# New orders, shorter MLP stages and constant products on TensorE in a transformer block for 16 sequences

## The chip, the cores and the metric

One core of one Trainium2 chip. The metric is the device time of one execution in microseconds. The engines are TensorE (PE; its weight loads are PEld), VectorE (DVE), ScalarE (ACT), GpSimd (POOL) and SyncE (SP), which here only issues DMAs.

## The reference, cut to what matters

For each of 16 samples x is 256 positions by 256 channels, with 16 heads of depth 16. Three residual blocks are modulated by a condition vector, and a fourth attends to the context:

```
m = silu(cond) @ w_ada + b_ada                       # 9 vectors of 256
h = ln(x) * (1 + sc) + sh;  x += g * (self_attn(h) @ w_so + b_so)    # "w": windows of 128, rolled by 64
h = ln(x) * (1 + sc) + sh;  x += g * (topk_attn(h, ctx) @ w_co + b_co)  # "t": softmax over the 16 largest of 256
h = ln(x) * (1 + sc) + sh;  x += g * (silu(h @ a) * (h @ b)) @ w_m2   # "m": 256 -> 2 x 1024 -> 256
x = x + attn(ada_ln(x), ada_ln(ctx)) @ Wp + bp        # "l": all 256 keys
```

## The kernel before

Nothing loops over the samples in the program order of an engine. Each sample is cut into some 230 stages, each stage belongs to one engine, and each engine runs its stages in an order that `orders()` sorts out of tables written by hand or by a planner: WINDOW (w), TOP (t), MIDDLE (m), LAST (l) and WEIGHTS give every stage a tick, `starts()` gives each sample its offset in each table, and SHIFTS moves single stages of samples 0 to 2 and 12 to 15. The ticks are only used for sorting. Semaphores hold the dependencies, so an order decides who waits, and not what is computed. In the middle of the run four samples are in work at once: the window part of sample b+1, the top-k part of b, the MLP of b-1 or b-2 and the last attention of b-3.

The stages that matter here, with the letter of the block behind the name and the number of the piece behind a colon:

- SP: `wd` weight chunk in, `xi` x in (three DMAs), `in_q`/`in_k` the stacks for the scores (six DMAs each), `gg` the guard row, `xo` out.
- PE: `wp` products with the condition (fp32), `x4` turns the normed x, `pj`, `vj` projections (12 products), `a` scores (4 or 8 products) into the bank pair `both_a`, `gd` turns the row maxima, `b` turned scores into `both_b` (for t with eight more products that add the `far` masks), `o` attention times values (fp32, 16 records in the profile), `ot`, `bk`, `xt` turns, `pr` output projection, `m1` and `m2` the MLP.
- DVE: `rm` row maximum of a score stage (1,024 columns at once, "pair instruction"), `t1` the eight largest and their removal for one bank, `t2` the next eight, `nv` division, `xa` residual add, `bn` statistics, `wl` the low part of a weight.
- ACT: `sp` scale and split into two fp16 halves, `e` exp over both banks of `both_b` ("pair instruction"), `os`, `fo`, `v`, `gc` copies, `mt`, `mh` of the MLP, `wh` the high part of a weight.
- POOL: `rs` norm, `lo` low half of a split, `fx` mask, `mp`, `ml` of the MLP.

`both_a` is one pair of banks for all score stages: stage n waits for `a_free >= 2 * (n - 1)`, which the last `rm` or `t1` on the one before gives. `t1:2k` and `t1:2k+1` read score stage `a_t:k`. The work banks (ND = 3) are taken in turn by `d_take`, in the order of TensorE's stages. `m1` has four stages a sample, each with two work banks and 24 products; `m2_0` has one stage of 48 products which waits for all four pieces of the hidden layer:

```
pe.wait_ge(hid_hi, HC // 2 * (b + 1))
pe.wait_ge(hid_lo, HC // 2 * (b + 1))
```

Weight chunks go through seven staging slots at first and later through three; the DMA of chunk i waits for the `wl` of the chunk that had its slot. `bank_c` is the bank of the `o` stages, of which they use the first 256 columns.

Of the kernel before, what the change touches and what calls it, by code (L numbers as in the profile page):

```python
# [12 lines left out]
P = 128  # L13
# [21 lines left out]
def by_depth(a, n):  # L35
# [11 lines left out]
    ("sp", "xi:0@-145.94128 in_wq:0@-27.37744 in_wk:0@-18.47637 gg_w:0@3.5209 gg_w:1@4.07101 gg_w:2@6.27184 "  # L47
            "gg_w:3@22.21006"),
    ("pe", "x4_n1:0@-9.09677 pj_wq:0@-1.98612 pj_wk:0@2.68519 vj_w:0@4.89993 a_w:0@24.58239 a_w:1@27.56313 "
            "gd_w:0@29.69328 gd_w:1@29.69488 a_w:2@30.1805 gd_w:2@33.0072 a_w:3@36.06898 b_w:0@37.52571 "  # L50
            "o_w:0@40.25652 b_w:1@40.44455 gd_w:3@40.44981 b_w:2@43.51234 o_w:1@45.50942 o_w:2@48.14002 "
            "b_w:3@48.47732 o_w:3@52.15513 ot_w:0@52.96945 bk_w:0@54.60357 pr_w:0@60.64486 xt_w:0@63.46943"),
    ("act", "sp_n1:0@-4.9099 sp_wq:0@0.03668 sp_wk:0@4.57516 v_w:0@7.99085 gc_w:0@30.25034 gc_w:1@31.91219 "
            "gc_w:2@35.31827 e_w:0@37.88181 os_w:0@39.82438 e_w:1@40.8623 gc_w:3@41.86752 e_w:2@45.6085 "
            "os_w:1@47.66581 os_w:2@49.63704 e_w:3@51.50998 os_w:3@53.88078 sp_ws:0@58.08033 fo_w:0@63.15316"),
    ("dve", "bn_n1:0@-31.7132 rm_w:0@25.42137 rm_w:1@27.82458 rm_w:2@29.82325 rm_w:3@36.91164 nv_w:0@56.27724 "
            "xa_w:0@66.96972"),
    ("pool", "rs_n1:0@-16.61517 lo_n1:0@-3.0515 lo_wq:0@3.04638 lo_wk:0@12.34686 lo_ws:0@60.30093"),
# [3 lines left out]
    ("sp", "ct:0@-99.6594 in_tk:0@-34.30848 in_tq:0@-24.27719 gg_t:0@14.98362 gg_t:1@23.54712 gg_t:2@34.21064 "  # L62
            "gg_t:3@52.14972"),
    ("pe", "pj_tk:0@-8.41414 x4_n2:0@1.63472 pj_tq:0@6.08886 a_t:0@23.94792 a_t:1@34.1613 a_t:2@40.7968 "
            "gd_t:0@41.76883 a_t:3@45.25534 b_t:0@45.59387 vj_t:0@51.57878 b_t:1@51.66042 gd_t:1@53.13278 "
            "a_t:4@54.9192 b_t:2@58.34345 a_t:5@59.57596 o_t:0@63.86381 gd_t:2@66.1775 a_t:6@67.38364 "
            "b_t:3@67.58863 o_t:1@71.25909 b_t:4@73.82902 a_t:7@75.59749 gd_t:3@81.92041 b_t:5@82.0796 "
            "b_t:6@86.37541 o_t:2@87.8269 b_t:7@88.51516 o_t:3@91.75181"),
# [1418 lines left out]
```

## Time and profile before

| | |
|---|---|
| three runs | 1408.02, 1410.12, 1412.46 us, median 1410.12 |
| the profiled execution | 1412.02 us; its span, first to last instruction, is 1409.4 us |
| mean granted TensorE clock | 0.951 |
| busy share of the span | PE 86%, DVE 82%, ACT 71%, POOL 62%, PEld 60% |
| products on TensorE | 13192 |

The span is the time of the traced instructions; 2.6 us of the execution lie around it. The page of the profile cuts the span in 40 slices of 35.2 us, and for each gives the busy share of each engine in tenths and the clock that TensorE was granted, in tenths of full speed (2.4 GHz; 5 would be 1.2 GHz throughout). The busy shares of the whole are means over a start, a long middle and an end which differ, so they are to be read by stretch.

### The profile page before, as it was taken

To read this page: it belongs to the slowest core of one execution; us is meant where nothing else is said; L and a number is where in the kernel's file an instruction comes from. 1 tells how busy PE (TensorE), PEld (TensorE's weight loads), DVE (VectorE), ACT (ScalarE), POOL (GpSimd) and SP (SyncE) were. 2 spreads that over 40 slices of the span, in tenths; PEclk is the share of its full clock that TensorE was granted. 3 is DMA by queue.
4 is the path that set the end of the run, shared out by engine and by line. 5 is a ranking of instruction groups with operands and counts; after the bars stand their busy time and mean duration, and the time that the engine had idled before them with its cause. 6 is when DMAs were issued, how large, how long until landed. Compare 5 with 4: busy or idle time off the path is not lost. (4 is left out here: it accounts for less than half of the span.)

```text
span 1409.4 us, 37816 instructions
## 1 busy us (share of the span) xinstructions
PE 1206.5 (86%) x13192; PEld 838.9 (60%) x13192; DVE 1155.1 (82%) x3823; ACT 994.4 (71%) x2001; POOL 878.4 (62%) x1161
## 2 busy tenths in 40 slices
PE   4647688989999999999999999999999989878765
PEld 4534365757666666666675766666666666555532
DVE  4339798989999999999999999999999999894322
ACT  3434476869687887869686969788787868576643
POOL 1133376958677685858585867768585848575610
PEclk9667799999999999999999999999999999999986
DMA  5411111202112120302021111112120211000010
GB/s 203 129 47 45 39 35 36 69 24 53 41 42 60 40 62 13 86 12 74 19 70 32 50 51 44 50 39 69 27 60 19 54 36 45 20 24 23 17 31 16
DMA packets 111385, 67.17 MB, mean 48 GB/s; under 512 B 13836, under 2 KB 107870, under 8 KB 111198
## 3 DMA queue, kind: packets, MB, share of 16 engines
q1 hardware_dynamic: 111198, 64.76, 17.1%
q8 instruction: 107, 1.75, 0.5%
q14 instruction: 80, 0.66, 0.2%
HBM read 22.33 MB, written 4.19 MB: 19 GB/s over the span
## 5 line engine op out<-in xcount | busy, mean ns | idle before, releaser
L1210 ACT ACTIVATE prob<-turned_score 128x1024 f32<-128x1024 f32 x320 | 326.5, 1020 | 113.3 <-PE turned_score L920 109.3
L1437 POOL TENSOR_TENSOR pair<-full,pair 128x512 f16<-128x512 f32 x192 | 221.7, 1159 | 154.8 <-ACT pair L1184 151.0
L1443 POOL TENSOR_SCALAR far<-far 128x512 bf16<-128x512 bf16 x256 | 158.0, 617 | 131.1 <-DVE far L1372 114.4
L1355 DVE MAX8 top<-score 128x8 f32<-128x256 f32 x512 | 193.5, 420 | 26.6 <-PE score L920 26.1
L1358 DVE MATCH_REPLACE8 rest<-top,score 128x256 f32<-128x256 f32 x512 | 208.3, 415 | 0.0
L1372 DVE MATCH_REPLACE8 far<-best,rest 128x256 bf16<-128x256 f32 x512 | 205.7, 410 | 0.2 <-issue 0.2
L1345 DVE TENSOR_REDUCE rowmax_l<-score 128x4 f32<-128x1024 f32 x128 | 156.2, 1220 | 54.2 <-PE score L920 40.8
L920 PE MATMUL work<-pair_n,w_m_hi 128*128 128x256 f16 x1024 | 172.7, 274 | 0.9 <-ACT other L1240 0.7
L920 PE MATMUL work<-pair_n,w_m_lo 128*128 128x256 f16 x512 | 140.1, 274 | 0.0
L1184 ACT ACTIVATE pair<-full 128x512 f16<-128x512 f32 x192 | 121.0, 630 | 23.6 <-DMA q_stack_l<-pair 6.6
L1422 POOL TENSOR_SCALAR rstd_n<-mean_var_n 128x2 f32<-128x2 f32 x64 | 12.8, 200 | 175.2 <-DVE mean_var_n L1337 172.6
L1345 DVE TENSOR_REDUCE rowmax_w<-score 128x8 f32<-128x1024 f32 x64 | 78.1, 1220 | 40.2 <-PE score L920 29.8
L920 PEld LDWEIGHTS work<-pair_n,w_m_hi 128*128 128x128 f16 x1024 | 98.0, 98 | 18.6 <-issue 6.3
L1365 DVE MAX8 best<-rest 128x8 f32<-128x256 f32 x256 | 107.0, 418 | 0.0
L1367 DVE MAX8 best<-rest 128x8 f32<-128x256 f32 x256 | 104.8, 410 | 0.0
L920 PE MATMUL work<-hid,w_m_hi 128*128 128x256 f16 x512 | 86.9, 277 | 1.2 <-issue 1.2
L1452 POOL TENSOR_TENSOR gated<-gated,linear 128x512 f32<-128x512 f32 x64 | 81.3, 1270 | 5.0
L1398 DVE TENSOR_TENSOR x_tile<-x_tile,work 128x512 f32<-128x512 f32 x64 | 43.7, 683 | 49.2 <-PE work L917 40.1
L920 PE MATMUL turned_score<-ident,far 128*128 128x128 bf16 x1024 | 82.1, 225 | 0.0
L1449 POOL TENSOR_TENSOR linear<-linear,other 128x512 f32<-128x512 f32 x64 | 81.3, 1270 | 0.0
L1456 POOL TENSOR_TENSOR hid<-gated,hid 128x512 f16<-128x512 f32 x64 | 74.0, 1159 | 10.1 <-ACT hid L1250 7.1
L920 PE MATMUL score<-k_stack_l,q_stack_l 48*128 48x256 f16 x512 | 51.3, 279 | 31.5 <-DVE rowmax_l L1345 23.9
(197 smaller groups left out, 3149.6 us busy)
## 6 DMA issues: line engine op xcount, KB each, us to landing
q_stack_w<-pair SPq DMA_DIRECT2D x96, 64.0 KB, 2.3
k_stack_w<-pair SPq DMA_DIRECT2D x96, 64.0 KB, 2.3
k_stack_t<-pair SPq DMA_DIRECT2D x96, 64.0 KB, 2.3
q_stack_t<-pair SPq DMA_DIRECT2D x96, 64.0 KB, 2.3
k_stack_l<-pair SPq DMA_DIRECT2D x96, 64.0 KB, 2.3
q_stack_l<-pair SPq DMA_DIRECT2D x96, 64.0 KB, 2.3
ctx_t<-in_ctx_turned SPq DMA_DIRECT2D x16, 256.0 KB, 2.9
ctx_l<-in_ctx SPq DMA_DIRECT2D x16, 256.0 KB, 2.9
```

The lines of the kernel that those rows point to most:

```text
L920: return pe.matmul(o, lhsT, rhs, start=start, stop=stop)
L1184: act.activation(pair_tile(s, b)[:, 0, :, :], tile[:, :, :], ACT.Copy).then_inc(split_hi, 1)
L1210: act.activation(prob[:, at:at + 2, :], both_b[:, :, :], ACT.Exp).then_inc(exp_done, 1)
L1345: dve.tensor_reduce(rowmax[s][n % 2][:, :].rearrange("p (z m) -> p z m", z=2)[:, :, at:at + wide], both_a[:, :, :].rearrange("p z (h k) -> ...
L1355: first = [step(dve.max(eight[:, t, :], bank[:, t * L:(t + 1) * L])) for t in range(LT)]
L1358: m = dve.match_replace(rest[p % 2][:, t, :], eight[:, t, :], bank[:, t * L:(t + 1) * L], -FAR)
L1365: second = [step(dve.max(best[p % 2][:, 0, :], rest[p % 2][:, 0, :]))]
L1367: second.append(step(dve.max(best[p % 2][:, 1, :], rest[p % 2][:, 1, :])))
L1372: m = dve.match_replace(far[p % NFAR][:, t, :], best[p % 2][:, t, :], rest[p % 2][:, t, :], -FAR)
L1437: pool.tensor_tensor(pr[:, 1, :, :], whole[:, :, :], pr[:, 0, :, :], ALU.subtract).then_inc(split_lo, 1)
L1443: pool.tensor_scalar(tile, tile, FAR, -1.0, ALU.add, ALU.mult).then_inc(far_fixed, 1)
L1449: pool.tensor_tensor(linear[:, two, :], linear[:, two, :], other[:, two, :], ALU.mult).then_inc(pair_product, 1)
```

## The change

1. All tables, `starts()` and SHIFTS have new numbers, so that the orders differ on all five engines; SHIFTS now is given for the same samples. No stage is added or taken away but for those of point 2.
2. `m1` is 8 stages with 12 products and one work bank each, `m2` is 4 stages of 12 products: two column halves for the first four of the eight depth chunks, then two for the rest. It takes its bank in the first of them, and a semaphore of its own, `m2_done`, tells of the last.
3. `idle_work()`: before 34 named stages TensorE multiplies `ident16` by itself into unused columns of `bank_c`, 821 times in all, behind a wait for the copy of the latest `o` stage. 553 of them are in the fill (119 before wp:14, 24 before the first x4, 45 before the first pj), 268 in samples 13 to 15.

Vector's order in one steady period before, from the `xa_w` of sample b to the next (@0 is sample b):

```
xa_w@0 t1:8@-1 t1:9@-1 bn_n2@0 rm_l:0@-3 t2:8@-1 t2:9@-1 t1:10@-1 t1:11@-1 rm_l:1@-3 t2:10@-1 t2:11@-1 t1:12@-1
t1:13@-1 t2:12@-1 rm_l:2@-3 t2:13@-1 rm_l:3@-3 rm_l:4@-3 nv_l@-4 rm_l:5@-3 t1:14@-1 t1:15@-1 t2:14@-1 rm_w:0@1
bn_nc@-1 rm_w:1@1 t2:15@-1 rm_w:2@1 xa_l@-4 bn_n1@2 t1:0@0 t1:1@0 t2:0@0 t2:1@0 rm_l:6@-3 rm_w:3@1 xa_m@-2 bn_n4@-2
nv_t@-1 rm_l:7@-3 t1:2@0 t2:2@0 t1:3@0 t2:3@0 t1:4@0 xa_t@-1 t1:5@0 bn_n3@-1 nv_w@1 t2:4@0 t2:5@0 t1:6@0 t1:7@0
t2:6@0 t2:7@0
```

and after:

```
xa_w@0 t1:9@-1 t2:8@-1 rm_l:0@-3 bn_n2@0 t2:9@-1 t1:10@-1 t1:11@-1 t2:10@-1 rm_l:1@-3 t2:11@-1 t1:12@-1 t1:13@-1
rm_l:2@-3 rm_l:3@-3 t2:12@-1 rm_l:4@-3 nv_l@-4 rm_l:5@-3 t2:13@-1 t1:14@-1 t1:15@-1 t2:14@-1 rm_w:0@1 t2:15@-1
rm_w:1@1 xa_l@-4 rm_w:2@1 bn_nc@-1 t1:0@0 t1:1@0 t2:0@0 rm_l:6@-3 t2:1@0 rm_w:3@1 xa_m@-2 nv_t@-1 bn_n4@-2
rm_l:7@-3 bn_n1@2 t1:2@0 t1:3@0 t2:2@0 t2:3@0 t1:4@0 xa_t@-1 bn_n3@-1 t1:5@0 nv_w@1 t2:4@0 t2:5@0 t1:6@0 t1:7@0
t2:6@0 t2:7@0 t1:8@0
```

In the fill, SP's order begins `wd:0 .. wd:9 xi:0 wd:10 ..` before and `wd:0 .. wd:13 xi:0@0 wd:14 .. wd:18 xi:0@1 wd:19 in_wq in_wk` after; VectorE's has `bn_n1` behind wl:5 before and behind wl:13 after; TensorE's has wp:14 behind `pj_wq` and wp:19 behind `a_w:2` before, and wp:14 in front of `x4_n1` and wp:19 in front of `a_w:0` after. At the end TensorE's order after has `m2:2 m2:3` of sample 14 between `b_t:7` and `o_t:3` of sample 15, where `m2_0` stood, and `m1:2` of sample 15 between `a_l:0` and `a_l:1` of sample 14.

The diff without the tables:

```diff
+IDLE_WORK = ("wp:0:14=119 x4_n1:0:0=24 pj_wq:0:0=45 wp:0:19=21 a_w:0:2=21 bk_w:0:0=18 pr_w:0:0=7 xt_w:0:0=17 "
+             "x4_n2:0:0=24 pj_tq:0:0=45 a_w:1:0=30 a_w:1:2=21 a_t:0:0=31 a_w:1:3=20 bk_w:1:0=25 pr_w:1:0=43 "
+             "a_t:0:4=10 a_t:0:7=25 a_t:1:0=7 bk_t:15:0=10 x4_n4:14:0=15 xt_t:15:0=17 a_l:14:3=15 bk_l:13:0=8 "
+             "xt_m:15:0=17 x4_n4:15:0=34 pj_lq:15:0=17 a_l:15:0=26 bk_l:14:0=8 a_l:15:3=9 a_l:15:7=14 "
+             "o_l:15:3=17 bk_l:15:0=18 pr_l:15:0=43")
...
-                   ("x4", "pj", "vj", "gd", "ot", "bk", "pr", "xt", "m1", "m2", "wp")]
-        d_keys = [k for k in d_users for _ in range(2 if k[0][:2] in ("ot", "m1") else 1)]
+                   ("x4", "pj", "vj", "gd", "ot", "bk", "pr", "xt", "m1", "wp") or k[0] == "m2" and k[2] == 0]
+        d_keys = [k for k in d_users for _ in range(2 if k[0][:2] == "ot" else 1)]
...
+            idle, o_begun = idle_work(), 0
             for piece, b, i in plan["pe"]:
                 kind, _, s = piece.partition("_")
+                if (piece, b, i) in idle:
+                    if o_begun > 0:
+                        pe.wait_ge(osum_done, o_begun)
+                    for _ in range(idle[piece, b, i]):
+                        mm(bank_c[:, L:L + P], ident16[:, :], ident16[:, :], True, True)
...
-                    for j in range(2):
-                        bank, n = d_take(piece, b, i, back=1 - j), 2 * i + j
-                        three_terms(bank[:, 0:L], W["m1"], slice(n * P, (n + 1) * P), own_pair["n3"], CC)
-                        m = three_terms(bank[:, L:2 * L], W["m1"], slice(HID + n * P, HID + (n + 1) * P),
-                                        own_pair["n3"], CC)
+                    bank = d_take(piece, b, i)
+                    three_terms(bank[:, 0:L], W["m1"], slice(i * P, (i + 1) * P), own_pair["n3"], CC)
+                    three_terms(bank[:, L:2 * L], W["m1"], slice(HID + i * P, HID + (i + 1) * P), own_pair["n3"],
+                                CC).then_inc(d_ready, 1)
+                elif kind == "m2":
+                    if b == 0 and i == 0:
+                        pe.wait_ge(lo_done, weight_count("m2"))
+                    c, half = i % 2, i // 2
+                    pe.wait_ge(hid_hi, HC // 2 * b + 2 * half + 2)
+                    pe.wait_ge(hid_lo, HC // 2 * b + 2 * half + 2)
+                    bank = d_take(piece, b, i) if i == 0 else d_bank("m2", b, 0)
+                    for k in range(HC // 2 * half, HC // 2 * (half + 1)):
+                        for n, (a, part) in enumerate((("hi", 0), ("hi", 1), ("lo", 0))):
+                            m = mm(bank[:, c * L:(c + 1) * L], W["m2"][a][:, k, c * P:(c + 1) * P], hid[:, part, k, :],
+                                   i == 0 and k == 0 and n == 0, i == 3 and k == HC - 1 and n == 2)
+                    if i == 0:
                         m.then_inc(d_ready, 1)
-                elif kind == "m2":
-                    if b == 0:
-                        pe.wait_ge(lo_done, weight_count("m2"))
-                    pe.wait_ge(hid_hi, HC // 2 * (b + 1))
-                    pe.wait_ge(hid_lo, HC // 2 * (b + 1))
-                    bank = d_take(piece, b, i)
-                    for c in range(CC):
-                        m = three_terms(bank[:, c * L:(c + 1) * L], W["m2"], slice(c * P, (c + 1) * P), hid, HC)
-                    m.then_inc(d_ready, 1)
+                    if i == 3:
+                        m.then_inc(m2_done, 1)
```

## Rows read from the trace of the kernel before

**Rows 1.** The page, the span in 40 slices: VectorE's busy tenths and TensorE's clock
```profile
DVE  4339798989999999999999999999999999894322
...
PEclk9667799999999999999999999999999999999986
```

**Rows 2.** The table by stretch: length, busy us of each engine, clock, DMA
```profile
42.00:69.30 27.30, 16.25 (x164) 12.25 (x164) 10.58 (x16) 10.51 (x17) 3.62 (x7) 0.55 0.44 133
120.50:170.00 49.50, 35.10 (x323) 21.92 (x322) 42.17 (x161) 21.72 (x41) 19.45 (x29) 0.78 0.19 49
605.90:681.90 76.00, 71.17 (x826) 49.77 (x818) 70.78 (x237) 60.97 (x125) 54.75 (x73) 1.00 0.18 47
1352.00:1409.40 57.40, 33.87 (x248) 16.06 (x248) 13.18 (x16) 18.35 (x30) 4.78 (x5) 0.68 0.11 28
```

**Rows 3.** VectorE's timeline, steady part: start, us, what, idle before and its end
```profile
642.47 0.69 DVE L1398 TENSOR_TENSOR x_tile<-x_tile,work 128x512 f32<-128x512 f32 x1 [0.80 <-PE work L917]
...
654.47 1.22 DVE L1345 TENSOR_REDUCE rowmax_l<-score 128x4 f32<-128x1024 f32 x1 [0.56 <-PE score L920]
...
667.97 1.23 DVE L1345 TENSOR_REDUCE rowmax_l<-score 128x4 f32<-128x1024 f32 x1 [0.55 <-issue]
...
718.46 0.69 DVE L1398 TENSOR_TENSOR x_tile<-x_tile,work 128x512 f32<-128x512 f32 x1 [0.76 <-PE work L917]
```

**Rows 4.** TensorE's timeline, steady part, end of an m1 stage and after
```profile
1100.68 0.27 PE L920 MATMUL work<-pair_n,w_m_lo 128*128 128x256 f16 x1
1100.88 0.39 PE L920 MATMUL score<-k_stack_l,q_stack_l 48*128 48x256 f16 x4
1101.21 0.39 PE L920 MATMUL work<-pair,w_qkv_hi 128*128 128x256 f16 x2
```

**Rows 5.** Timelines of SP, VectorE and ScalarE, the first 45 us
```profile
15.74 1.70 SPq L869 DMA_DIRECT2D x_tile<-in_x  x3
23.59 0.97 SPq L864 DMA_DIRECT2D hid<-in_L_xcond_w_m  x2
...
30.12 0.37 SPq L864 DMA_DIRECT2D hid<-in_L_xcond_w_m  x1
...
40.54 3.88 SPq L889 DMA_DIRECT2D q_stack_w<-pair  x6
...
21.57 0.75 DVE L1334 BATCH_NORM_STATS2 stats_n<-x_tile 128x6 f32<-128x256 f32 x2 [2.74 <-DMA x_tile<-in_x]
...
31.35 0.55 ACT L1176 ACTIVATE full<-work,ada 128x256 f32<-128x256 f32 x1
```

**Rows 6.** TensorE's timeline, the fill
```profile
34.50 0.58 PE L920 MATMUL work<-pair,w_qkv_hi 128*128 128x256 f16 x2 [7.39 <-POOL pair L1437]
...
38.33 0.38 PE L920 MATMUL work<-pair,w_qkv_hi 128*128 128x256 f16 x2
...
50.11 0.61 PE L920 MATMUL score<-k_stack_w,q_stack_w 48*128 48x128 f16 x8 [2.11 <-DMA k_stack_w<-pair]
...
54.82 3.44 PE L920 MATMUL work<-cond_T,hid 128*128 128x16 f32 x16
...
101.47 0.61 PE L920 MATMUL score<-k_stack_t,q_stack_t 48*128 48x256 f16 x4 [1.47 <-DVE rowmax_w L1345]
```

**Rows 7.** The chain that ended last: start, us, what
```profile
1275.07 1.84 PE work L920 x14
1276.91 1.04 PE attended L920 x16
...
1280.85 5.24 PE work L920 x48
...
1383.12 1.87 PE attended L920 x16
...
1401.69 3.50 PE work L920 x14
```

**Rows 8.** VectorE's timeline, its last MATCH_REPLACE8
```profile
1275.77 0.41 DVE L1372 MATCH_REPLACE8 far<-best,rest 128x256 bf16<-128x256 f32 x1
```

More of the change, by code:

```diff
@@ L46 @@
 WINDOW = (
[L47 to L58, printed above, removed]
+    ("sp", "xi:0@-149.05811 in_wq:0@-22.39374 in_wk:0@-21.63518 gg_w:0@-6.70743 gg_w:1@-6.20742 gg_w:2@3.72515 "
+            "gg_w:3@10.37658"),
@@ L59 @@
+    ("dve", "bn_n1:0@-17.84269 rm_w:0@24.47919 rm_w:1@26.55546 rm_w:2@29.71092 rm_w:3@39.32701 nv_w:0@54.92831 "
+            "xa_w:0@62.38605"),
+    ("pool", "rs_n1:0@-19.44322 lo_n1:0@-8.8718 lo_wq:0@3.49632 lo_wk:0@11.63506 lo_ws:0@54.42283"),
 )
 TOP = (
[L62 to L68, printed above, removed]
@@ new lines @@
+    ("pe", "pj_tk:0@-7.66208 x4_n2:0@1.34278 pj_tq:0@10.7192 a_t:0@24.62457 a_t:1@36.3855 a_t:2@40.46992 "
+            "gd_t:0@41.16911 b_t:0@46.39389 a_t:3@47.54705 b_t:1@49.06852 vj_t:0@49.42558 gd_t:1@52.91429 "
+            "a_t:4@53.28068 b_t:2@59.66427 a_t:5@60.56827 o_t:0@62.91677 a_t:6@66.51438 b_t:3@67.69902 "
+            "gd_t:2@68.67071 o_t:1@76.5107 b_t:4@79.63426 a_t:7@80.32481 gd_t:3@82.46194 b_t:5@83.04624 "
+            "o_t:2@85.87755 b_t:6@86.53666 b_t:7@89.11422 o_t:3@92.86888"),
@@ L109 @@
-    ("pool", "rs_nc:0@-31.49787 lo_nc:0@7.97103 rs_n4:0@9.40636 lo_n4:0@19.15097 lo_lk:0@22.80535 lo_lq:0@24.22699 "
-            "lo_ls:0@124.61473"),
+    ("sp", "cl:0@-113.28517 in_lk:0@-11.3877 in_lq:0@-8.30312 gg_l:0@8.54748 gg_l:1@30.92847 gg_l:2@34.1449 "
+            "gg_l:3@55.14878 xo:0@129.90888"),
+    ("pe", "x4_nc:0@-16.97885 x4_n4:0@14.3594 pj_lk:0@18.74146 pj_lq:0@20.78305 a_l:0@36.38003 a_l:1@41.1725 "
+            "vj_l:0@42.70583 gd_l:0@42.73227 a_l:2@49.44513 a_l:3@50.22124 b_l:0@50.82866 a_l:4@52.16861 "
+            "b_l:1@53.17633 a_l:5@54.31746 gd_l:1@54.80942 o_l:0@58.38301 gd_l:2@64.72824 a_l:6@67.98034 "
+            "b_l:2@68.09437 b_l:3@72.88562 a_l:7@73.99668 o_l:1@76.59819 b_l:4@79.41849 b_l:5@83.66516 "
+            "gd_l:3@87.4598 o_l:2@91.66504 b_l:6@98.85371 b_l:7@105.14574 o_l:3@107.70126 ot_l:0@117.03745 "
+            "bk_l:0@119.19155 pr_l:0@125.23099"),
@@ L512, in shifts, with idle_work @@
             found[stage, b, int(item)] = float(tick)
+    return found
+IDLE_WORK = ("wp:0:14=119 x4_n1:0:0=24 pj_wq:0:0=45 wp:0:19=21 a_w:0:2=21 bk_w:0:0=18 pr_w:0:0=7 xt_w:0:0=17 "
[3 more added lines that the diff above has]
+             "o_l:15:3=17 bk_l:15:0=18 pr_l:15:0=43")
+def idle_work():
+    found = {}
+    for one in IDLE_WORK.split():
+        name, _, n = one.partition("=")
+        stage, b, item = name.split(":")
+        found[stage, int(b), int(item)] = int(n)
     return found
@@ L731, in build @@
         hid_lo = sem("hid_lo")
+        m2_done = sem("m2_done")
         dve_own = sem("dve_own")
```

796 lines of the change are left out of this document (406 added, 390 removed).

## The prediction, made blind

> **What bounds the kernel now.** I read the page's slices first [rows 1]. VectorE is at 7 to 9 tenths from the fourth slice to the fifth from the end, and the granted TensorE clock is below full in two places only: the first 170 us and the last 60. So there are three stages with different limits: a fill, a steady part, a drain. The table by stretch gives each its numbers [rows 2]. In a steady period of 76.0 us (the same addition to x_tile starts at 642.47 and 718.46 [rows 3]) VectorE is busy 70.8 us and TensorE 71.2. VectorE is what sets the period: its order leaves it idle 5.2 us, and TensorE's own idle time is mostly waiting for VectorE to give back the score banks. In the fill TensorE is busy 16.3 of 27.3 us at a clock of 0.55, and in the last 57.4 us it is busy 33.9 at 0.68, with the other engines far from full: there a chain of latencies counts, and TensorE's part of it runs at half speed.
>
> How long half speed makes a step: 12 products of the same shape begin 0.21 us apart at 34.50 and 0.11 us apart at 38.33 [rows 6]. (The clock column has no record before 38 us and so says 1.00 there; the pace says half.) An `o` stage of sample 15 takes 1.87 us where one at full clock takes 1.04, and `pr_l` 3.50 against 1.84 [rows 7].
>
> **The steady part, orders.** All score stages share one pair of banks. After VectorE's last reading of it, the next `a` stage runs and VectorE reads again; if VectorE has nothing else between, it waits: 0.56 us at 654.47, 0.55 at 667.97 [rows 3]. Counting in the orders of `orders()`: before, 5 of the 20 score stages of a period follow each other on VectorE with nothing between; after, 2 do. (`rm_l:1`, `rm_w:3` and `t1:2` get a `t2` or a `bn` in front.) At 0.55 us each that is -1.6 us a period. The wait of `xa_w` (0.80 us at 642.47 [rows 3]) has `t1:8`, 1.5 us of work, moved in front of it; it may go, or be covered in half: -0.4. Against it: `rm_l:2` now comes directly behind `t1:13`, while TensorE has between `a_t:6` and `a_l:2` an `o`, a `b_t`, an x4, two small turns and half of the old `m1` (1.04 + 0.9 + 0.4 + 0.2 + 1.3 us and the score itself, some 4.1 us) where VectorE has only two `t1`, 2.9 us. So about 0.6 us beyond an ordinary turnaround, and I put another 0.4 for similar overruns at `a_l:1`, `a_l:5` and `a_w:1`. Net -1.6 - 0.4 + 1.0 = -1.0 us a period. Twelve periods lie between the add of sample 3 and that of sample 15: -12 us. From both sides: no wait comes back and both savings are whole, -2.4 a period, -29 us; the new waits are as large again as I think and none of `xa_w` goes, +0.4 a period, +5 us.
>
> **The steady part, smaller stages.** `m1` becomes 8 stages of 12 products, `m2` 4 of 12. The products are the same 1,536 and 768, and inside a stage a half costs nothing extra. What costs is a change of tiling: from products of 128 rows to score products of 48 rows the next start comes 0.20 us after the last instead of 0.11, and again on the way back [rows 4]. The old order has 63 such changes in a period, the new one 72: 9 x 0.1 = 0.9 us of TensorE. It has 4.8 us idle in a period [rows 2], so 3.9 are left, and the cover is VectorE; without it the price is 0.9 us a period, 11 us in all. The Trainium skill ("TensorEngine Tiling (Array Packing)", section Key Properties) says that changing the tiling mode drains TensorE, and speaks so against cutting stages finer between scores; the trace agrees with 0.1 us a change, and by the rule alone, with TensorE on the path, these steps would be +11 us where I count nothing.
>
> **The fill.** Fillers: 553 of the 821 constant products stand in the stages of samples 0 and 1 and the weights. None is in the trace of before; the nearest row is the eight 128-column bf16 products of `b_t` (0.055 us apart, 0.9 us with their four wide ones), so 30 us at full clock, 60 at half, spread over pauses. Each filler is behind a wait for the latest osum, which the next `o` would make anyway.
>
> First the order. `xi:0` moves on SP from behind wd:9 to behind wd:13. Before it was issued at 15.74 and `bn_n1` began at 21.57; wd:13 was issued at 30.12 [rows 5]. With `bn_n1` out of the weights' way, wd:10 (23.59 before) can go some 2.5 us earlier and wd:13 at about 27.3. Then x0 is issued by 29 and lands near 33, 11.5 us later. Not all of that is loss: before, `sp_n1` stood behind three weight copies on ScalarE and began only at 31.35 [rows 5], and `pj_wq` at 34.50. After: bn 33, x4 37.4, sp_n1 38, pj_wq 41.3, at full clock now, then in_wq from 45.7 against 40.54 [rows 5]. The 12 issues of in_wq and in_wk and the landing come behind it as before, so `a_w:0` is at about 55.3 against 50.11 [rows 6]: +5.2. The 119 fillers ahead of wp:14 begin at about 24.4, last 7 to 13 us, and end before or close to the time x is normed (37).
> From there: wp:19, 3.4 us between `a_w:2` and `gd_w:2` [rows 6], is moved ahead of `a_w:0`: -3.1. The other TensorE steps of sample 0's window attention, 42 to 69 us, halve where they are on the chain (some 3.5 us of the 16.3 busy). In the next stretch at half speed, before 101 us, `x4_n2` and `pj_tq` halve: -1.7. `a_t:0`, where VectorE becomes full, moves by 5.2 - 3.1 - 3.5 - 1.7 = -3.1 from 101.47 [rows 6]. From 120.5 to 170 VectorE is idle 7.3 of 49.5 us, against 3.4 at the steady rate, with TensorE's clock at 0.78 [rows 2]; half of the excess goes with the clock, -2. Fill: -5. Bounds: +5 (x late by all of 5.2, fillers do not lift the clock), -11 (x costs nothing).
>
> **The drain.** It is the 133 us behind VectorE's last MATCH_REPLACE8 [rows 8]. `m2` of samples 14 and 15 was 48 products, 5.24 us, in one piece [rows 7]. For sample 14 it stood between the last `b_t` of sample 15 and its last `o_t`; only half of it stands there now: -2.6. For sample 15 it stood behind the last `ml`; now the first half runs while GpSimd is at the later quarters: -2.6. `m1:1` of sample 15 was behind two scores that waited for in_lq's landing; its halves are now around one: -1.5. Then the clock: in the last 57.4 us TensorE is busy 33.9 at 0.68 [rows 2]. Summed over the chain, `pj_lq` 1.3, `pr_l` 1.7 twice, four `o` 0.8 each, `ot` 0.7, small ones 2: 10.6 us if all were at full clock. The 152 fillers of this stretch fill only parts of the pauses (26 products are 1.4 us in a wait of five), so I take half, -5. Drain: -12. Bounds: -4 (one half of `m2`, no clock, 43 fillers before the last `pr_l` 1.8 us too long at half clock) and -19.
>
> On the clock altogether there is a second estimate, which the sum does not use. The Trainium skill ("TensorE: Matmul & The Clock Gate", section Terms) prices throttled time at time x (1 - K/N); with the mean clock of 0.951 that is 69 us for the whole kernel, so up to -69 were TensorE always on the chain and all of it won. This trace does not agree that it all counts: TensorE is busy only 60% of such stretches [rows 2].
>
> **Sum.** The profiled execution took 1412.0 us, its span is 1409.4; the median of the three runs is 1410.1, 1.9 less. 1412.0 - 12 - 5 - 12 = 1383.0, less 1.9: 1381.
>
> **Rivals.**
> 1. *Only the ends gain.* The steady order trades five turnarounds for overruns and tiling changes, and the period stays at 76.0. For it: VectorE's and TensorE's loads are equal to 0.4 us, so every stage moved earlier makes another later. Against: the adjacent waits are plain in the rows. 1410 - 17 = 1393.
> 2. *The fillers do not lift the clock and only the order gains.* For it: they are in short groups, and the clock stayed at 0.55 with TensorE 60% busy. Against: the longest, 119 and 24 and 45, stand where TensorE was empty for 7.4 us. Fill +5, drain -7, steady -12: 1396.
> 3. *Slower: TensorE becomes the bound of the period.* Its work goes to 72.1 us; with stages that wait for their inputs at the head of its queue, scores come late for VectorE. It decides from +1.4 us a period, when 12 periods eat the 17 us of the ends; at +2.3 the time is 1410 - 17 + 28 = 1421. For it: 5.2 us of VectorE's idle time is already waiting for TensorE. Against: three more of the twenty scores have cover on VectorE than before, and `o_l:3`, 1 us of TensorE, now stands behind `a_t:6` and no longer in front of it.
> 4. *The whole gain.* -2.4 a period, -11 and -13 at the ends: 1357.
>
> **How the numbers follow.** The forecast 0.50; rival 1 0.17, rival 2 0.10, rival 3 0.14, rival 4 0.09. The likeliest alone spans 1368 to 1392. Leaving out most of rival 3 and the far side of rival 4 gives 1357 to 1405. 0.3%, 4 us, is what a measurement can tell from no change. Slower is rival 3 with its point of decision passed, 0.11; within 0.3% is its remainder and the edge of rival 2, 0.06; faster the rest, 0.83.
>
> **What would show it.** Right: a steady period of 75 us, VectorE's waits before `rm_l:1`, `rm_w:3`, `t1:2` and `xa_w` gone and one of about 1 us before `rm_l:2`; the first window score near 55 us but `a_t:0` near 98; a clock near 1 from about 30 us to 170 us; a last stretch, from the last MATCH_REPLACE8 to the end, of 121 us against 133. Wrong: a period of 76 or more, `a_t:0` after 101, or a clock in the last 57 us still under 0.8.

## The result, and the profile after

The changed kernel takes 1349.97 us (median of four runs, 1343.52 to 1354.03) where the kernel before takes 1409.54 beside it: ratio 0.957 [0.953, 0.961]. Run once more in a later comparison it took 1348.1 (five runs, 1342.23 to 1352.33), ratio 0.954 [0.951, 0.957]. So it is 60 us faster, where I predicted 29 and where my range ended at 1357. The profiled execution, the fastest of the first four, has a span of 1341.7 us and a mean granted clock of 0.977. It is set against the 1409.4 us span of before; some 8 of those 68 us are chance, since this execution was 6.4 us under the median of its kernel and that of before 2.5 over.

The page of after, its 40 slices (of 33.5 us); for [rows 1]:

```profile
DVE  4418999989999999999999999999999999896322
...
PEclk9888999989999999999999999999999999999998
```

The same stretches by event, first in before, then in after: up to the first top-k score `a_t:0`, to the residual add `xa_w` of sample 3, to that of sample 15, to VectorE's last MATCH_REPLACE8, to the end. The columns are length, then busy us of PE, PEld, DVE, ACT and POOL with their instructions, granted clock, DMA share and GB/s.

```profile
0.00:101.50 101.50, 55.01 (x400) 44.55 (x402) 35.30 (x71) 38.36 (x65) 23.82 (x40) 0.79 0.42 131
101.50:262.10 160.60, 123.67 (x1329) 85.29 (x1330) 143.58 (x544) 95.37 (x192) 88.34 (x123) 0.86 0.15 39
262.10:1178.20 916.10, 851.93 (x9792) 597.76 (x9789) 851.89 (x2845) 728.50 (x1488) 656.72 (x865) 1.00 0.18 46
1178.20:1276.20 98.00, 84.40 (x876) 56.30 (x877) 89.89 (x312) 67.82 (x137) 66.84 (x84) 0.97 0.08 21
1276.20:1409.40 133.20, 91.49 (x802) 54.98 (x799) 34.40 (x55) 64.39 (x121) 42.65 (x52) 0.85 0.09 23
```

```profile
0.00:104.90 104.90, 75.93 (x821) 67.91 (x822) 35.79 (x71) 38.13 (x65) 20.49 (x35) 0.89 0.43 132
104.90:255.50 150.60, 124.56 (x1462) 88.25 (x1461) 144.22 (x549) 96.08 (x193) 90.45 (x127) 0.94 0.14 38
255.50:1129.70 874.20, 849.75 (x9775) 593.88 (x9775) 841.50 (x2839) 725.89 (x1480) 651.06 (x858) 1.00 0.19 48
1129.70:1228.20 98.50, 88.73 (x942) 58.91 (x939) 91.19 (x314) 71.05 (x146) 71.77 (x93) 0.98 0.10 26
1228.20:1341.70 113.50, 94.32 (x1024) 65.82 (x1022) 33.68 (x51) 63.62 (x119) 41.41 (x51) 0.95 0.10 25
```

Read the first column down: +3.4, -10.0, -41.9, +0.5, -19.7 us (the last boundary of after lies 0.2 us early, so the last two are nearer +0.7 and -19.9). In the other profiled execution of the changed kernel, 1352.33 us long, the same five are +8.3, -6.3, -39.4, -0.1 and -21.4. So 60 to 67% of the gain is in the twelve periods of the middle, where the mean clock is 0.99 to 1.00 before and after; the fill differs by 5 to 9 us between the two profiles. And the first stretch became *longer*, though its clock went from 0.79 to 0.89 (0.83 in the other profile).

One steady period of after on VectorE, from `xa_w` to where the next has already begun; every line with a wait before it stands here, so this is all that is left of [rows 3]:

```profile
618.62 0.68 DVE L1439 TENSOR_TENSOR x_tile<-x_tile,work 128x512 f32<-128x512 f32 x1
...
636.67 1.22 DVE L1386 TENSOR_REDUCE rowmax_l<-score 128x4 f32<-128x1024 f32 x1 [0.86 <-issue]
638.46 1.23 DVE L1386 TENSOR_REDUCE rowmax_l<-score 128x4 f32<-128x1024 f32 x1 [0.56 <-PE score L947]
...
654.99 1.23 DVE L1386 TENSOR_REDUCE rowmax_w<-score 128x8 f32<-128x1024 f32 x1 [0.38 <-PE score L947]
```

These are `rm_l:2`, `rm_l:3` and `rm_w:2`, 1.8 us together; the period is 72.1, and in before it was 76.0 with 5.1 us of waits. The 3.3 us of waits that went are most of the 3.9. The other 0.6 us wasn't traced; an estimate is that six waits fewer save some 0.5, since an instruction of VectorE that doesn't wait starts about 0.08 us before the last one is over (a row maximum takes 1.22 us and the next starts after 1.14). What VectorE waited for over four periods, before and then after (total us, times, longest):

```profile
DVE top L1355 <- PE score L920: 6.7, 12, 0.7
DVE x_tile L1398 <- PE work L917: 4.6, 8, 0.8
DVE rowmax_l L1345 <- PE score L920: 2.4, 4, 0.8
DVE rowmax_w L1345 <- PE score L920: 2.2, 4, 0.6
DVE rowmax_l L1345 <- issue: 2.2, 4, 0.5
DVE recip L1386 <- PE work L917: 2.1, 4, 0.5
```

```profile
DVE rowmax_l L1386 <- issue: 3.7, 4, 1.1
DVE rowmax_l L1386 <- PE score L947: 2.2, 4, 0.6
DVE rowmax_w L1386 <- PE score L947: 1.5, 4, 0.4
```

20.2 us became 7.4. Not only waits for a score went: the adds (`xa_w`, `xa_t`) and the divisions (`nv`) waited 6.7 us for TensorE's products and wait no more. TensorE's side of the same four periods, before and after:

```profile
PE score L920 <- DVE rowmax_l L1345: 9.0, 20, 0.8
PE turned_score L920 <- ACT prob L1210: 3.8, 11, 0.7
PE score L920 <- DVE rowmax_w L1345: 1.7, 4, 0.4
```

```profile
PE work L944 <- POOL normed L1471: 2.6, 4, 0.7
PE work L944 <- DVE attn L1431: 1.1, 3, 0.6
```

In before TensorE stood 24 times in these four periods in front of a score because VectorE's row maximum of the last one wasn't done; in after not once. The two engines had been waiting for each other by turns.

### The profile page after: what moved, and what is told of

It is laid out like the page before. It is cut to its first block and busy times, and to the rows that moved or that the text cites. A ratio compares the mean times of both kernels' runs of the same rounds, so it can differ in the third digit from the quotient of the medians.

```text
span 1341.7 us, 39506 instructions
## 1 busy us (share of the span) xinstructions
PE 1233.3 (92%) x14013; PEld 874.8 (65%) x14013; DVE 1146.4 (85%) x3819; ACT 994.8 (74%) x2001; POOL 875.2 (65%) x1161
## 3 DMA queue, kind: packets, MB, share of 16 engines
q1 hardware_dynamic: 111198, 64.76, 17.9%
## 5 line engine op out<-in xcount | busy, mean ns | idle before, releaser
L1386 DVE TENSOR_REDUCE rowmax_w<-score 128x8 f32<-128x1024 f32 x64 | 78.0, 1219 | 36.7 <-PE score L947 19.7
L1406 DVE MAX8 best<-rest 128x8 f32<-128x256 f32 x256 | 106.7, 417 | 0.0
L947 PEld LDWEIGHTS turned_score<-ident,far 128*128 128x128 bf16 x1024 | 58.6, 99 | 27.8 <-issue 26.0
```

The costliest lines, as they stand in the source:

```text
L947: return pe.matmul(o, lhsT, rhs, start=start, stop=stop)
L1386: dve.tensor_reduce(rowmax[s][n % 2][:, :].rearrange("p (z m) -> p z m", z=2)[:, :, at:at + wide], both_a[:, :, :].rearrange("p z (h k) -> ...
L1406: second = [step(dve.max(best[p % 2][:, 0, :], rest[p % 2][:, 0, :]))]
```

## Experiments

Stages are given as in `orders()`; moves are for all steady samples. A period is the distance of the same `xa_w` add in two samples. "Run 3" is the experiment with number 3. Times are medians, with the ratio to the kernel before beside it and its 95% interval; the medians of before lay between 1409.85 and 1411.99.

**1. The constant products taken out, and only those of the end taken out.**

```diff
-            idle, o_begun = idle_work(), 0
+            idle, o_begun = {}, 0                                                    # e1
+            idle, o_begun = {k: n for k, n in idle_work().items() if k[1] < 3}, 0    # e2
```

> The changed kernel without its 821 constant products; orders and MLP stages stay. If the constant products hold the clock up and that is worth about a fifth of the gain, the steady period stays at 72.1 us, the clock in the fill and in the last 57 us falls back to 0.6 to 0.7, and the time rises by 8 to 15 us, to 1358 to 1365. Rival: the orders gave the ends as well, the constant products only fill waits, and the time stays within 4 us of 1350.

> The changed kernel with the constant products of samples 0 to 2 and the weights alone. Theory A (each end gains by its clock): about 4 us slower than the changed kernel, the last stretch at half clock as it is without any of them, from t2:15 to the end 119 us instead of 115. Theory B (the latency chain of the drain doesn't feel the clock): within 2 us of the changed kernel.

> The changed kernel once more, beside the next three on one chip. It gave 1349.97 us (1343.52 to 1354.03). Theory A (the constant products are worth the 12 us that its profiled execution shows beside the one without them): its median here lies 8 us or more under 1354.2. Theory B (they are worth 4 us, and the one profiled execution was a good one): 1348 to 1352.

Without any 1354.23 us (0.958 [0.956, 0.961]), with those of the fill alone 1354.45 (0.961 [0.958, 0.963]), with all 1348.1 and 1349.97. So the constants are worth 4 to 6 us of the 60 by the medians, all of it at the end, and 2 to 6 by the ratios; the interval without them overlaps both intervals with them, so the size is not well known. The stretch from the last `t2` to the end is 119.5 us without them and 114.8 with. In the fill the first top-k score comes earlier in some executions only. This is `a_t:0` of the same kernel in its other profiled execution:

```profile
109.82 0.39 PE L947 MATMUL score<-k_stack_t,q_stack_t 48*128 48x256 f16 x4
```

109.8, as late as without any constants (109.85), where the first profile had 104.9. Of the profiles here that share this start and these constants, seven have `a_t:0` at 104.5 to 106.7 and four at 108.1 to 109.8; with the constants of the fill alone it is at 109.55.

**2. The new orders with every MLP piece back in one place.** `m1:4` and `m1:5` adjacent, and all of `m2` where `m2:3` stands.

> The changed kernel with the pieces of the MLP put back together on TensorE: m1 0 and 1, 2 and 3, 4 and 5, 6 and 7 stand directly behind each other, and so do the four of m2, in the place of the last. If the smaller stages are what lets TensorE serve the scores in time, the steady period goes back by 2 us or more of the 3.9 won (74 to 76 us, time 1375 to 1395). If the order of VectorE did it, the period stays within 0.8 us of 72.1, and only the end loses up to 5 us: 1350 to 1364.

1429.70 us, ratio 1.012 [1.010, 1.015]: slower than before, with a period of 78.5. VectorE's waits over four periods:

```profile
DVE rowmax_w L1414 <- issue: 21.9, 4, 5.9
DVE rowmax_l L1414 <- PE score L975: 7.5, 5, 1.8
```

`rm_w:3` waits 5.1 to 5.9 us each time: all of `m2`, 5.2 us, stands in front of its score. That was too coarse a test (the place was the wrong one), so the next two put the pieces together one kind at a time and in the better place.

**3. `m2` whole in front of `a_l:6`; `m1` in pairs.**

```diff
+    for b in range(1, B - 3):                                    # m2 whole
+        pieces = [("m2", b, n) for n in range(4)]
+        at = order.index(("m2", b, 1))
...
+        order[at:at + 1] = pieces
...
+        for n in (0, 2, 4, 6):                                   # m1 in pairs, another run
+            order.remove(("m1", b, n))
+            order.insert(order.index(("m1", b, n + 1)), ("m1", b, n))
```

> The changed kernel with m2 in one piece again for samples 1 to 12, in the place of its second piece, in front of a_l:6. Between a_t:0 and a_l:6 TensorE then has about 6.4 us of work where VectorE has 4.4. If it is the TensorE work between two scores that must fit into VectorE's work between them, rm_l:6 waits 2 us and the period goes to 74: 1370 to 1378. If only the place in the run before last mattered (the pieces pushed a_w:3 back there), the period stays at 72.1: 1350.

> The changed kernel with only m1 in pairs again (m1:4 directly in front of m1:5, behind a_l:2). By the same rule rm_l:2 waits less by up to 0.9 us and rm_l:3 more by 1.3 us, so the period is 72.1 to 72.9 and the time 1350 to 1360: m2's pieces carry the gain and m1's hardly anything. Rival: both matter alike, 1365 or more.

`m2` whole: 1375.63 (0.976 [0.973, 0.979]), period 74.0, a new wait of 1.86 us before `rm_l:6`. `m1` in pairs: 1357.32 (0.962 [0.960, 0.965]), period 72.8, `rm_l:3` waits 1.84 instead of 0.56 and `rm_l:2` 0.55 instead of 0.87. In the new orders cutting `m2` is worth 26 to 28 us and cutting `m1` 7 to 9, where I had put both at nothing in the middle.

**4. The covers in the old orders.** The kernel before, with `rm_l:1` behind `t2:10`, `t2:1` behind `rm_l:6` and `bn_n1` behind `rm_l:7`, which is what the change does on VectorE with the three covers I priced.

```diff
+    turned("dve", ("rm_l", 1), ("t2", 10), -2)
+    turned("dve", ("t2", 1), ("rm_l", 6), 3)
+    behind("dve", ("bn_n1", 0), ("rm_l", 7), 5)
```

> The kernel before with three moves on VectorE alone, in all samples: rm_l:1 behind t2:10, t2:1 behind rm_l:6, bn_n1 behind rm_l:7, so that three score stages get work between them and the one before. If each uncovered turnaround costs its 0.55 us, the steady period falls from 76.0 to 74.4 and the time by 19 us, to 1390. Rival: the wait only goes elsewhere, since TensorE is the one that is late; period 75.5 to 76.5 and time within 5 us of 1410.

1440.91, ratio 1.019 [1.016, 1.022]: 29 us *slower* than before, with a period of 78.5. Over four periods:

```profile
DVE top L1375 <- PE score L940: 13.1, 12, 2.1
DVE rowmax_l L1365 <- issue: 11.3, 8, 2.3
DVE x_tile L1418 <- PE work L937: 4.7, 8, 0.8
DVE recip L1406 <- PE work L937: 2.5, 4, 0.7
```

The three turnarounds are gone, and `rm_l:6` waits 2.27, `t1:12` 2.13 instead of 0.69, and `t1:4` 0.65. The first has a plain reason: all of `m2`, 5.2 us of TensorE, stands in front of the score of `rm_l:6`, and the move took `t2:1`, 1.46 us of VectorE, from in front of it.

**5. The two heads in the old orders**: `t1:8` in front of `xa_w`, `a_t:6` in front of `o_l:3`.

> The kernel before with two swaps, in the steady samples: t1:8 of sample b-1 in front of xa_w of sample b on VectorE, and a_t:6 in front of o_l:3 on TensorE. They aim at the waits of 0.78 us (before xa_w) and 0.69 us (before t1:12). If they simply go, the period falls to 74.5 and the time by 18 us, to 1392. Rival: something behind them waits instead; then the period stays within 0.5 us of 76.0.

1410.24, ratio 0.998 [0.997, 1.000], period 75.8: the waits before `xa_w` and `t1:12` went, and 0.70 before `rm_l:0` and 0.65 before `rm_l:2` came.

**6. The new code with the old orders**: `m1` and `m2` pieces side by side where the whole stages stood, only `a_l:6` between the halves of `m2`, no constants; then the same with the moves of 4 and 5.

> The orders of before with m1 and m2 in pieces that stay together, but a_l:6 between the halves of m2 in the steady samples; no constant products. VectorE had work enough in front of rm_l:6 already, so by the rule of what fits between two scores the period stays at 76.0, at best 75.5: 1400 to 1412. If the small pieces gain by themselves, 1390 or less.

> The same with the three moves on VectorE and the two swaps of the runs before, which gave +2 % and nothing without the pieces. If pieces and order only pay together, rm_l:6 no longer waits 2.3 us and t1:12 no longer 2.1: the period falls to 74 or 75 and the time to 1380 to 1398, well under the kernel before. If the moves are bad in themselves, it stays over 1420.

1411.24 (1.001 [1.000, 1.003]) and 1417.71 (1.006 [1.004, 1.008]), periods 76.2 and 76.3. Neither the code of the small stages nor these moves with it bring anything in the old orders. But the pieces take back 23 of the 29 us that the covers of run 4 cost: with `a_l:6` inside `m2`, `rm_l:6` no longer waits and `t1:12` waits 1.13, while `rm_w:3` waits 1.24.

**7. The covers taken off in the new orders**, the mirror of 4.

```diff
+    turned("dve", ("t2", 10), ("rm_l", 1), 2)
+    turned("dve", ("rm_l", 6), ("t2", 1), -3)
...
+        order.remove(("bn_n1", b, 0))
+        order.insert(order.index(("t1", b - 2, 0)), ("bn_n1", b, 0))
```

> The changed kernel with the three covers taken off on VectorE alone: rm_l:1 in front of t2:10, t2:1 in front of rm_l:6, bn_n1 back in front of t1:0. Theory 1 (the prediction's: a score stage that follows its neighbour directly costs 0.55 us): +1.6 us in each of 12 periods, 1370, a period of 73.8. Theory 2 (a cover is worth what TensorE's work between two score stages exceeds VectorE's between their readings, counted in the new order): rm_l:1 moved off t2:10 leaves 4.4 us of TensorE's work against 2.9, +1.2 at rm_l:1; the place before rm_l:6 is 3.8 us against 5.8, nothing, but rm_w:3 then waits 3.0 against 1.1, +1.5; rm_l:7 to t1:2 2.2 against 1.1, +0.8: +3 us or more a period, 1385 or more, a period of 75.

1377.81 (0.976 [0.973, 0.979]), period 74.4 to 74.8. The same three moves that cost 29 us in the old orders are worth 28 to 30 in the new ones. Theory 2 had the direction and the places, but was 7 us too high: `rm_l:1` waits 1.4 to 1.6, and `rm_w:3` and `t1:2` only 0.55 and 0.62.

**8. The two heads taken back in the new orders, alone and with the covers.** `t1:8` behind `xa_w`, `bn_n3` behind `t1:5`.

> The changed kernel with t1:8 behind xa_w and bn_n3 behind t1:5 again, on VectorE alone. Theory 1 (the work in front hides the late products): the 0.77 us before xa_w and the 0.37 before xa_t come back, +1.1 a period, 1362, a period of 73.2. Theory 2 (TensorE's products for them come earlier by themselves, as it waits less for the score banks): less than 0.3 a period comes back, 1348 to 1353.

> The changed kernel with the three covers off and the two heads back (t1:8 behind xa_w, bn_n3 behind t1:5), on VectorE alone. Theory 1 (the late products before xa_w, nv_w and xa_t follow from TensorE's own waits): with TensorE waiting 4.7 us a period as without the covers, the waits before xa_w and its like are 0.5 us or more, a period of 75 or more, 1386 or more. Theory 2 (they come from the order of other engines): at most 0.2 us before them, a period of 74.4 as without the covers, 1376 to 1381.

Alone 1353.93 (0.959 [0.956, 0.961]), the period 72.2 nearly as it was, 0 to 0.28 us before `xa_w` in place of the 0.77 of before; the 4 to 6 us over the changed kernel are not in the period, and the intervals overlap. With the covers off too 1377.96 (0.976 [0.974, 0.978]), against 1377.81 without: again nothing, with 0 to 0.41 before `xa_w`. So it isn't mainly the work in front that removed the waits of the adds; TensorE's products for them come earlier against VectorE in the new orders, even with both engines waiting for each other again (4.2 us a period on VectorE).

**9. Two moves with a price by counting**: `t2:12` from `rm_l:4` to `rm_l:2`; `o_l:3` back in front of `a_t:6`.

> The changed kernel with t2:12 in front of rm_l:2 and no longer in front of rm_l:4. The largest wait left, 0.86 us before rm_l:2, gets 1.46 us of work in front. Theory 1 (each wait by itself): rm_l:2 0, rm_l:4 0.55, rm_l:3 0.59 as before: -0.3 a period, 1345. Theory 2 (a count of both engines' work between score stages, carried from one to the next): rm_l:4 waits 0.84 and rm_l:5 0.51, rm_l:3 0.5: +0.8 a period, +9 us, 1358.

> The changed kernel with o_l:3 in front of a_t:6 on TensorE again. Theory 1 (each by itself): t1:12 waits for the 1.25 us of o_l:3, rm_l:2 no longer waits: about +0.4 a period, +5 us. Theory 2 (the count, carried on): TensorE has 0.26 us and what it is ahead at a_t:6, the work is the same up to a_l:2, so the period moves by less than 0.15 and the whole by less than 2 us.

1350.51 and 1349.50 (both 0.955, [0.953, 0.958]), periods 72.35 and 72.28. The second is as counted: `t1:12` waits 0.59 again and `rm_l:2` 0.55 instead of 0.87. In the first the waits stand where the count put them (`rm_l:4` 0.72, `rm_l:5` 0.49, `rm_l:3` 0.56, none at `rm_l:2`), but cost 0.25 a period and not 0.8, so its 1358 was 7 to 8 us too high.

**10. The edits of runs 3, 7 and 8 together**: covers off and heads back, `m2` whole, `m1` in pairs, in the otherwise new orders.

> The changed kernel with covers and heads undone, and m2 in one piece and m1 in pairs besides. Theory 1 (each is a price of its own): +2.4 +1.9 +0.7 a period, 77.1, 1410. Theory 2 (the count of both engines' work between two score stages): undone covers put t2:1 in front of rm_l:6, which then covers the whole of m2, so m2 costs nothing more and m1 1.3 at rm_l:3: 75.7, 1393 to 1397.

1415.97 us, ratio 1.003 [1.001, 1.004]: 5 us longer than before. The twelve periods take 930.2 us, 56 more than in after and 14 more than in before; the last stretch keeps its gain (114.6), as `m2` stays cut in the last three samples:

```profile
263.90:1194.10 930.20, 859.62 (x9771) 601.05 (x9768) 846.76 (x2843) 725.39 (x1481) 651.89 (x859) 0.99 0.17 46
1303.90:1418.50 114.60, 93.22 (x1027) 65.28 (x1024) 34.00 (x53) 63.64 (x119) 41.78 (x51) 0.97 0.10 25
```

So with these few edits undone the whole gain of the middle is gone; that they don't carry it by themselves is what run 6 suggests, where they stand in the old orders. Of the eight periods up to sample 11 five are 75.0 to 76.4 us, theory 2's 75.7, and three are 77.4 to 77.8, theory 1's 77.1 and over. `a_l:2` waits 2.2 to 2.5 us for VectorE in all eight. What is new in the three is that right behind this wait the clock is halved for 3.4 us, so that the pair of `m1` behind it begins a product every 0.21 us instead of every 0.11, and `rm_l:3` waits 3.3 to 3.5 us, where it is 1.84 in most of the others. TensorE's timeline in one of the three, and the table of the 3.4 us:

```profile
742.37 0.39 PE L985 MATMUL score<-k_stack_l,q_stack_l 48*128 48x256 f16 x4 [2.36 <-DVE rest L1437]
...
743.11 0.63 PE L985 MATMUL work<-pair_n,w_m_hi 128*128 128x256 f16 x2
...
746.66 0.38 PE L985 MATMUL work<-pair_n,w_m_hi 128*128 128x256 f16 x2
```

```profile
743.00:746.40 3.40, 3.40 (x18) 2.42 (x17) 1.08 (x1) 1.17 (x4) 2.01 (x3) 0.51 0.30 77
```

The time of 1416 is nearer to theory 1's 1410 than to theory 2's 1393 to 1397, but the waits speak for theory 2: `rm_l:6` doesn't wait at all, so whole `m2` costs nothing here, and in the periods without a fall of the clock `rm_l:3` waits 1.84, 1.3 more than in after. What theory 2 lacked are the falls of the clock, seven in the twelve periods, six of them at this place at some 1.6 us each (an estimate from the wait of `rm_l:3`), and 11 us between the add of sample 15 and the last MATCH_REPLACE8, 109.8 us against 98.3, which no count covered.

**11. The old order of the start, on all engines**, with the constants set before the stages that now wait (80 before `pj_wq`, 40 before wp:17, 30 before `a_w:0`, 12 each before `x4_n1` and `a_w:2`), and the same without constants.

```diff
+    for engine, text in FIRST.items():      # FIRST: the stages of before up to o_w:3 of sample 0
...
+        found[engine][:len(first)] = first
```

> The changed kernel with the old order of its start on all engines, so that the first x is loaded, normed and projected as early as before, and with constant products in front of the stages that now wait. Theory 1 (the late x cost some 5 us and nothing behind it gives them back): the first top score 5 to 7 us earlier than 104.9, the last scores of the window as much earlier, the whole 1344 to 1346. Theory 2 (the fill is bound by the weights and GpSimd's work, not by x): the first top score within 1.5 us of 104.9, the whole within 2 us of the changed kernel.

> The changed kernel with the old order of the start and no constant products at all. Against 1342.6 with them and 1354.3 with the new start and none. Theory A (the start's order gives 5 to 7 us, the constants 4 to 6): 1347 to 1350. Theory B (the old start gains only because its constants stand in better places): 1354. First window score at 50, first top score at 102 to 103 at half clock.

1342.61 us (1341.53 to 1344.07), ratio 0.952 [0.950, 0.954], and without constants 1349.74 (0.956 [0.953, 0.958]). Without constants the old start is 4.5 us better than the new one (1354.23), though the two intervals overlap; with them 5.5 to 7.4, and this is the lowest median of all. `a_t:0` is 4.3 us earlier than in the first profile of the changed kernel and 9.2 earlier than in the second. Its stretches to `a_t:0` and from the last `t2` to the end, and then those without constants:

```profile
0.00:100.60 100.60, 73.96 (x764) 65.96 (x764) 34.86 (x71) 38.41 (x65) 22.07 (x35) 0.86 0.44 138
...
1227.20:1339.70 112.50, 92.92 (x1044) 64.66 (x1036) 34.97 (x57) 63.72 (x119) 42.59 (x52) 0.98 0.11 27
```

```profile
0.00:102.00 102.00, 57.20 (x397) 45.77 (x397) 35.48 (x71) 38.62 (x65) 22.05 (x35) 0.77 0.45 135
...
1225.00:1345.10 120.10, 87.66 (x784) 53.24 (x776) 35.49 (x57) 63.71 (x119) 42.90 (x53) 0.83 0.10 25
```

Constants take the clock of the fill from 0.77 to 0.86 and give 1.4 us up to `a_t:0`, of which nothing is left at `xa_w` of sample 3 (255.6 with, 255.5 without); at the end they take the clock from 0.83 to 0.98 and give 7.6. Each is one execution.

## Why the prediction was wrong

**The step that failed is the price of the orders in the steady part**, "-1.6 -0.4 +1.0 = -1.0 us a period" and with it the bound "-2.4 a period". It was -3.5 a period over the twelve (-41.9; -3.3 in the other profile), and -3.9 in the quiet middle. Three things were wrong in it.

First, the sum netted five turnarounds against two before it priced the bound. Set side by side, the two orders say more than the 5 and the 2. All five turnarounds of before get work in front, `rm_l:4` and `t1:14` too (from `t2:12` and `t2:13`), which the prediction doesn't name, and two new ones arise, `rm_l:2` and `rm_l:3`. So "no wait comes back" would have been five times 0.55 and 0.8, 3.5 us a period by the prediction's own price, and not 2.4. And other waits stood in no term: `t1:12` (0.69; `o_l:3` moved from in front of its score), `xa_t` (0.36) and the divisions (0.53) are 1.6 us a period in before and gone in after. As a list of waits in us a period:

| | predicted | measured |
|---|---|---|
| turnarounds, five of before to two | -1.6 | -1.6 (2.69 gone, 0.56 and 0.55 come) |
| beyond a turnaround at `rm_l:2`, and elsewhere | +1.0 | +0.7 (0.32, and 0.37 at `rm_w:2`) |
| `xa_w` | -0.4 | -0.8 |
| `t1:12`, `xa_t`, the divisions | 0 | -1.6 |

That is -3.3 of the 3.9. That `t1:12` follows from `o_l:3` is shown by run 9, which brings 0.59 of it back, though the period moves by only 0.2; run 8 shows that the waits of the adds don't follow from the work in front of them on VectorE. What in the orders of TensorE, ScalarE and GpSimd took those away, and the waits of the divisions, wasn't separated, since each order is tied to the others'. That stays open, and so does what the moves of `t2:12` and `t2:13` are worth: run 9 moves only the first, and to another place.

Second, a wait that stands adjacent is not a price. The same three covers cost 29 us in the old orders (run 4) and are worth 28 to 30 in the new ones (run 7), where I had -1.6 us a period for them; by run 7 they are 2.5. A score stage can begin when VectorE has read the one before, and VectorE can read it when TensorE has come to it. What counts is TensorE's work from one score stage to the next against VectorE's work from one reading to the next, and what TensorE is ahead is carried on to the next pair. Put the row maxima at 1.14 us from start to start, a `t1` or `t2` at 1.46, a score at 0.5 until it can be read, and TensorE's stages at their distances in the trace, and follow both orders by those two rules. Such a count is an estimate. Made after the result, it gives a period of 71.8 for after (72.1 measured), 73.6 for run 7 (74.4 to 74.8), 73.5 and 73.1 for run 3 (74.0 and 72.8), 72.6 and 71.9 for run 9 (72.35, 72.28), and the waits in the right places. In the old orders it gives 73.3 for before (76.0), 74.2 for run 4 (78.5), 73.7 for run 6 (76.2): it has run 4 slower than before, but 2.5 to 4.3 us a period are missing. The other engines, which it leaves out, are a candidate; no run shows it. Where the count was used ahead of a run, it had the places of the waits, and times 7 to 8 us too high in runs 7 and 9 and some 20 too low in run 10.

Third, "smaller stages: nothing". Its cost was right to leave out: with 9 more changes of tiling TensorE is busy 71.0 us in a period, where it was 71.2 in before, and not 72.1. But the gain was left out too. A stage of 5.2 us between two scores can't be covered by 4.4 us of VectorE's work, and halves can: 1.9 us a period for `m2`, 0.7 for `m1` (run 3), only in orders that have the room (run 6). The Trainium skill ("TensorEngine Tiling (Array Packing)", section Key Properties) says that a change of the tiling mode drains TensorE. No run here prices that alone; what the finer cut gave between scores was larger than what the extra changes cost.

**Point by point.** *What bounds the kernel*: VectorE sets the period, right but half of it; TensorE waited 24 times in four periods for VectorE, so both did. *Turnarounds 5 to 2*: right, `rm_l:1`, `rm_w:3`, `t1:2` and `xa_w` no longer wait; the new wait before `rm_l:2` was put at about 1 us and is 0.86. The "similar overruns" of 0.4 are one of 0.38 at `rm_w:2`, a place that I hadn't named.

*Fill, -5*: -6.6 to `xa_w` of sample 3 in this profile, which is luck: in the other one of the same kernel it is +2.0, and +2.7 without constants. `a_w:0` at 55.3 was nearly right (56.0 and 58.5). From there to `a_t:0` I took off 8.3 us (wp:19 3.1, clock 3.5 and 1.7), and 2.4 came in the first profile and 0.1 in the second, so `a_t:0` is at 104.9 and 109.8 and not at 98.4; "`a_t:0` after 101" was one of my signs of being wrong. The clock was not near 1 from 30 to 170 us either, but 0.81 from 42 to 69.3 and 0.93 from 120.5 to 170:

```profile
55.97 0.61 PE L947 MATMUL score<-k_stack_w,q_stack_w 48*128 48x128 f16 x8 [6.50 <-DMA k_stack_w<-pair]
...
65.01 0.27 PE L944 MATMUL work<-ident,rowmax_w 128*8 128x128 f32 x1 [0.77 <-DVE rowmax_w L1386]
65.21 0.64 PE L947 MATMUL attended<-prob,v_w 128*32 128x128 f32 x16
66.36 1.08 PE L947 MATMUL attended<-prob,v_w 128*32 128x128 f32 x16 [0.50 <-ACT osum_w L1253]
67.37 0.61 PE L947 MATMUL turned_score<-q_stack_w,k_stack_w 49*128 49x128 f16 x8
69.13 0.61 PE L947 MATMUL turned_score<-q_stack_w,k_stack_w 49*128 49x128 f16 x8 [1.14 <-ACT prob L1248]
```

The second `o` at 66.36 takes 1.08 us where the first took 0.64: the clock had fallen again, and no constants stand there. The wp:19 term didn't show: without constants `a_w:0` to `a_t:0` is 51.1 us, against 51.4 in before, though other stages moved as well and no run moves wp:19 alone. What made up for it lies behind `a_t:0`: the new orders hold from sample 1 on, and from there to `xa_w` of sample 3 it is -10.0 (-6.3 in the other profile, -5.6 without constants), where I had counted -2.

*Drain, -12*: -19.7. The clock's -5 was right (4.7 by run 1, 7.6 in run 11). The orders' -6.7 was less than half of some 15: `o_t:3` of sample 15 comes 5.2 us sooner after the last `t2` and not 2.6; from the first `m1` to `fo_m` of sample 15 it is 29.8 us against 36.6, -6.8, where I had -4.1; and the last attention became 3.4 us shorter even without constants, where I had none. The chain of after, where the 5.24 us of [rows 7] stood and at the last piece of `m2`, and its end:

```profile
1229.79 0.77 PE turned_score L947 x12
1230.56 2.63 PE work L947 x24
...
1278.65 1.00 PE attended L947 x16
1279.86 2.63 PE work L947 x24
```

```profile
1335.55 2.02 PE work L947 x14
```

Half an `m2` each time, as said, and `pr_l` takes 2.02 against 3.50. The three parts make up the 15 us of the orders; why they are larger than what I had put on them wasn't taken apart further.

**The rivals.** Rival 1 (only the ends gain) fell with the period of 72.1. Rival 2 was half right: in the fill the constants lift the clock a little and shorten the chain unreliably. Rival 3, TensorE as the bound, didn't come about; in the new orders its waits over four periods went from 17.9 to 3.9 us. Rival 4 was nearest, and still 7 us too slow, since it rested on the same -2.4. The estimate by the Trainium skill ("TensorE: Matmul & The Clock Gate", section Terms), up to -69 us for all throttled time, doesn't hold as a price here. With all constants gone the records at half clock add up to 151 us, instead of 63 and 87 in the two profiles with them, and the time is 4 to 6 us longer.

## What to carry to other kernels

Compare two orders position by position before netting them: five pairs gone and two new ones is not three pairs gone. Where two engines alternate on one set of banks, price an order by counting both engines' work between two hand-overs, with the lead carried on, and not by the adjacent pairs of one engine; the same moves were worth 28 us in one order and cost 29 in another. Here the count gave the places of the waits, and periods within about 1 us in the new orders but 2.5 to 4.3 short in the old. Waits that stand in no term of the sum are not a floor: they may come from the other engine's queue. Cut the longest stage between two hand-overs until the partner's work covers it, and hold the clock up by constant work only where a single chain is on TensorE, at the end rather than in the fill.

## What the runs showed of the hardware beyond that

The granted clock differs between executions of one kernel where TensorE is loaded with gaps: the changed kernel's records at half clock sum to 63 us in one profile and 87 in another, `a_t:0` is at 104.9 and 109.8, and the mean clock of its runs goes with their time (0.968 at 1352.33 us, 0.980 at 1342.23). And it can fall in the middle of a nearly full stretch: in run 10 it fell eight times between 500 and 1,220 us, for 3.4 us each, and seven of the eight begin right at `a_l:2`, behind its wait of 2.1 to 2.9 us. In three other periods of the same stretch, at 666, 820 and 1,055 us, the same wait of 2.1 to 2.4 us stands without a fall, so the wait alone doesn't decide it. Of the two profiles of the changed kernel, one has a clock of 1.00 from 294 to 1,212 us and the other fell to half for 6.8 us at 1,098, inside a wait of TensorE of 1.9 us. So a wait of TensorE can cost more than its own length, but not each time: at this place in run 10 `rm_l:3` waits some 1.6 us longer in the periods with the fall than in those without.
